# A rotated tile's stack filled by three reads of 32 rows, and the first maxima sent before the last two query tiles

## The reference

```python
q = _apply_rope(q, cos, sin)
k = _apply_rope(k, cos, sin)
k_h = jnp.repeat(k, GROUP_SIZE, axis=1)
v_h = jnp.repeat(v, GROUP_SIZE, axis=1)
scores = jnp.einsum('bhqd,bhkd->bhqk', q, k_h) / math.sqrt(HEAD_DIM)
scores = jnp.where(causal[None, None], jnp.finfo(scores.dtype).min, scores)
attn = jax.nn.softmax(scores, axis=-1)
ctx = jnp.einsum('bhqk,bhkd->bhqd', attn, v_h)
```

## Time and profile before

| | before |
|---|---|
| median of 3 runs | 604.18 us (604.08 to 607.48) |
| the profiled execution | 602.86 us, span 601.1 us |
| mean granted TensorE clock | 0.936 |
| TensorE busy (matmuls) | 475.4 us, 79% |
| VectorE busy | 364.4 us, 61% |
| ScalarE busy | 300.8 us, 50% |
| POOL busy | 280.6 us, 47% |
| DMA moved | 50.83 MB, mean 85 GB/s |

### The profile page before, as it was taken

The page is one execution under the profiler, slowest core; times in us unless marked ns, Lnnn a source line. Parts: engine busy times, 40 slices in busy tenths (PEclk is TensorE's granted clock), DMA queues, the critical chain, the costliest instruction groups (busy, mean ns, idle before and its releaser), DMA issues.

```text
span 601.1 us, 9842 instructions
## 1 busy us (share of the span) xinstructions
PE 475.4 (79%) x3986; PEld 264.5 (44%) x3986; DVE 364.4 (61%) x620; ACT 300.8 (50%) x300; POOL 280.6 (47%) x153
## 2 busy tenths in 40 slices
PE   2678987593069899999995888898889999966777
PEld 2356733241035455555552455454444544435433
DVE  5776366673016676676663566687557676767436
ACT  2644224200057556677664577767762641455433
POOL 4030115332037778988886367666773534220000
PEclk9899989797569899999999899999999999997699
DMA  8623264322210111111114022222229110000015
GB/s 327 226 89 99 73 216 152 121 69 71 80 34 11 37 34 41 37 45 46 45 38 130 12 89 91 89 89 89 78 101 332 53 36 17 1 2 1 19 52 213
DMA packets 20424, 50.83 MB, mean 85 GB/s; under 512 B 4248, under 2 KB 9496, under 8 KB 19096
## 3 DMA queue, kind: packets, MB, share of 16 engines
q1 hardware_dynamic: 19080, 41.69, 20.3%
q10 hardware_dynamic: 1296, 8.45, 4.1%
HBM read 40.57 MB, written 9.44 MB: 83 GB/s over the span
## 4 chain that ended last, share of the span: by engine, by line
PE 40%; DVE 16%; ACT 15%; DMA 13%; issue 12%; POOL 2%; SPq 1%; ACTq 0%; DVEq 0%; POOLq 0%
ACT s1reg L510 8%; PE ps L1263 8%; PE ps L1129 6%; PE ps L1191 4%; PE ps L1210 4%; PE ps L1398 4%; DMA qstack<-mrow 4%; DMA rope_scratch<-s1reg 3%; PE ps L1355 3%; PE ps L1171 3%; DVE stat L706 3%; DVE mt L762 2%; DMA qstack<-rope_scratch 2%; PE ps L1157 2%; DMA s1reg<-in_weights 2%
## 5 line engine op out<-in xcount | busy, mean ns | idle before, releaser
L762 DVE TENSOR_REDUCE mt<-ps 128x1 f32<-128x512 f32 (+3 forms) x176 | 107.2, 637 | 118.7 <-PE ps L1173 118.1
L510 ACT ACTIVATE s1reg<-ps 128x1280 f32<-128x1280 f32 x64 | 78.7, 1229 | 67.5 <-PE ps L1193 66.7
L1129 PE MATMUL ps<-xT,wqx 128*128 128x512 f16 x384 | 98.0, 393 | 7.1 <-DVE s1reg L753 7.1
L1191 PE MATMUL ps<-qstack,kreg 98*128 98x512 f16 (+3 forms) x256 | 59.3, 309 | 54.0 <-DMA qstack<-mrow 28.5
L1263 PE MATMUL ps<-wo_reg,xT 128*128 128x512 f16 x384 | 93.1, 383 | 7.8 <-DVE wqx L790 6.9
L1171 PE MATMUL ps<-kreg,qstack 96*128 96x512 f16 (+3 forms) x256 | 67.2, 309 | 10.3 <-DMA qstack<-rope_scratch 6.5
L1059 POOL TENSOR_TENSOR s1reg<-s1reg 128x1280 f16<-128x1280 f32 x19 | 49.8, 2629 | 33.8 <-ACT s1reg L516 33.8
L1191 PEld LDWEIGHTS ps<-qstack,kreg 98*128 98x128 f16 x256 | 25.5, 100 | 82.0 <-ACT s1reg L510 33.9
L1129 PEld LDWEIGHTS ps<-xT,wqx 128*128 128x128 f16 x384 | 36.2, 101 | 47.1 <-issue 14.0
L1263 PEld LDWEIGHTS ps<-wo_reg,xT 128*128 128x128 f16 x384 | 35.7, 98 | 46.1 <-DVE wqx L790 7.1
L1059 POOL TENSOR_TENSOR wkv<-s1reg,wkv 128x1280 f16<-128x1280 f32 x18 | 46.9, 2615 | 19.3 <-ACT wkv L516 19.3
(11 more groups left out here) (128 smaller groups left out, 939.5 us busy)
## 6 DMA issues: line engine op xcount, KB each, us to landing
s1reg<-in_weights ACTq DMA_DIRECT2D x8, 1024.0 KB, 6.2
s1reg<-in_ctx SPq DMA_DIRECT2D x16, 512.0 KB, 4.7
rope_scratch<-s1reg SPq DMA_DIRECT2D x40, 128.0 KB, 2.5
qstack<-in_x SPq DMA_DIRECT2D x8, 512.0 KB, 5.4
qstack<-rope_scratch SPq DMA_DIRECT2D x16, 256.0 KB
s1reg<-in_x SPq DMA_DIRECT2D x16, 256.0 KB, 3.1
out<-s1reg SPq DMA_DIRECT2D x7, 512.0 KB, 2.7
s1reg<-in_L_ffn_weight SPq DMA_DIRECT2D x5, 512.0 KB, 5.8
```

What stands on the lines that cost most here:

```text
L510: nc.scalar.activation(ebuf[:, j % 2, :], st_ps[:, 0:SCORES], ACT.Exp, scale=EXP_SCALE, bias=P_LOG_SCALE).then_inc(e_done, 1)
L762: nc.vector.reduce_max(mt[:, G % 2, heads[0]:heads[-1] + 1, qt:qt + 1], ps[:, 3 + n % 2, 0:w * len(heads)].rearrange("p (h n) -> p h n", n ...
L1129: last = mm(out_ap, w(ws, k), xT[:, xs, KT * b + k, :], start=(k == 0 and n == 0), stop=(k == KT - 1 and n == 2))
L1191: mm(st_ps[:, SEG[k]:SEG[k] + n], kstack[0:ST_ROWS, one(G), P * k:P * k + P], qstack[0:ST_ROWS, one(slot + j), P * k:T], start=True, stop= ...
```

## The change

A stack is filled by three reads of 32 rows x 4 KB, one for each part, all of the form that so far only the last part had; `from_scratch` takes the list of the halves. The counts on `stack_ready` go from 32 to 48 for a tile. And `maxima(0)` stands ahead of tiles 10 and 11 on SyncE's queue, where it stood between them.

```diff
-            def from_scratch(n, to, slot, pair):
+            def from_scratch(n, to, slot, parts):
                 sp.wait_ge(scr_written[n % 2], 32 * (n // 2 + 1))
                 if n >= 2:
-                    sp.wait_ge(stack_ready[n % 2], 32 * (n // 2))
-                sp.dma_start(to[0:2 * DH, slot:slot + HG, :], pair).then_inc(stack_ready[n % 2], 16)
+                    sp.wait_ge(stack_ready[n % 2], 48 * (n // 2))
+                for part, hl in enumerate(parts):
+                    sp.dma_start(to[DH * part:DH * part + DH, slot:slot + HG, :], scr[n, :, hl, :, :]).then_inc(stack_ready[n % 2], 16)
 
             def k_stack(n):
-                from_scratch(n, kstack, HG * n, scr[n, :, 0:1, :, :].rearrange("r s h t -> s r (h t)").broadcast_to([2, DH, HG * T]))
-                sp.dma_start(kstack[2 * DH:QK_ROWS, HG * n:HG * n + HG, :], scr[n, :, 1, :, :]).then_inc(stack_ready[n % 2], 16)
+                from_scratch(n, kstack, HG * n, (0, 0, 1))
 
             def q_stack(n):
-                slot = (n - 4) % KV * HG
-                from_scratch(n, qstack, slot, scr[n, :, :, :, :].rearrange("r s h t -> s r (h t)"))
-                sp.dma_start(qstack[2 * DH:QK_ROWS, slot:slot + HG, :], scr[n, :, 0, :, :]).then_inc(stack_ready[n % 2], 16)
+                from_scratch(n, qstack, (n - 4) % KV * HG, (0, 1, 0))
...
-            to_scratch(10)
-            q_stack(10)
             maxima(0)
-            to_scratch(11)
-            q_stack(11)
+            for n in range(10, 12):
+                to_scratch(n)
+                q_stack(n)
...
-                    pe.wait_ge(stack_ready[G % 2], 32 * (G // 2 + 3))
+                    pe.wait_ge(stack_ready[G % 2], 48 * (G // 2 + 3))
```

## The result

| | before | changed |
|---|---|---|
| median of the runs | 604.13 us (604.01 to 607.48) | 561.41 us (559.44 to 561.94) |
| the profiled execution | 602.86 us, span 601.1 us | 559.44 us, span 557.6 us |
| mean granted TensorE clock | 0.936 | 0.971 |
| TensorE busy | 475.4 us | 472.1 us |

The ratio, which is estimated from all the runs, is 0.9275 (95% interval 0.9236 to 0.9313), so 43.8 us less, between 41.5 and 46.2; the two medians alone are 42.7 us apart. The forecast was 36.1 us less.

The account below looks back on a forecast made before the run. TensorE was taken to wait on the tiles' transport, paced by 64-row reads on two DMA engines. Gains of 25.3 + 9.3 + 1.0 + 0.5 = 36.1 us off 604.18 gave 568.1 us, range 561 to 580.

Parts of the forecast that it names:

- The two-engine read as the pace of the transport: SyncE's stack transport: the 64-row read runs on two DMA engines, 9.05 us a tile; three reads make it 5 us.
- 25.3 us for the maxima: TensorE's wait for the first row of maxima: goes in full, 25.3 us gained, with a cover of 2.5 us.
- Tile 4, 9.3 us: Rotation and stack waits at tile 4: 3.3 + 6.5 - 0.5 = 9.3 us gained, between 5 and 9.8.
- Clock, 1.0 us: After tile 4's 6.5 us pause: without it TensorE's clock is not lowered, 1.0 us gained, between 0 and 1.9.
- The first group, 0.5 us: First group after the maxima stall: 0.5 us gained of the 1.3 us it takes above a middle group.
- a group longer than 18 us: Sign of being wrong: any group taking over 18 us, where groups of 16.6 us were expected.
- Later groups: Groups after the first: reads are already issued behind the maxima and nobody waits for them, cost 0.
- only the order counts: Rival at the reads: time goes by bytes or rows, however spread; 8.7 us gained, 595 us, chance 0.04.
- slower: Rival at the reads: all three land on the same two engines; 7.8 us lost, 612 us, chance 0.02.
- Little changed: Rival at the reads: their fixed parts add up and spreading saves nothing; 3.6 us lost, 607.8 us, chance 0.01.
- the new wait at the maxima: Rival: maxima behind the reads, or VectorE, hold TensorE; 5 to 15 us given back, 577 to 590, chance 0.08.
- The range: Predicted total time: 561 to 580 us, holding the forecast and the start of the new-wait rival.

Follow-up runs that it names:

- wide 64-row read: Changed kernel with two reads a tile, 64 rows in one read from a scratch layout with outermost dimension 64, and one of 32: 560.08 us, ratio 0.9257.
- order-only run: Kernel before with the first maxima moved ahead of tiles 10 and 11, the 64-row reads kept: 598.67 us, ratio 0.9874.

## Why the prediction was right or wrong

- **The two-engine read as the pace of the transport**: right. Rate, share and collision came out, and the wide 64-row read shows it without the split. The pace fell to 4.4 us a tile, 5 were worked out.
- **25.3 us for the maxima**: right, the whole wait is gone. They left at 127.6 and landed at 130.1, and TensorE asked at 134.1; they were forecast to be ready at 125.8, to land by 130 and to be asked for at 132.5.
- **Tile 4, 9.3 us**: 6.5 measured (113.90 to 107.37). The load landed at 88.7 as forecast (88.4 to 89). TensorE asked for the stack at 104.7 instead of 104.1 and then waited 2.7 us instead of 0.5. The chain of waits of the changed kernel says where these come from:

```profile
94.79 1.17 POOL s1reg L1039
...
95.97 4.05 DMA rope_scratch<-s1reg
...
100.86 6.46 DMA qstack<-rope_scratch
```

The long add cost less against the forecast than it looks: POOL's low half, counted with the 2.74 us of the kernel before, took 1.17 us and ended at 95.95 instead of 95.4. The larger miss is the landing of the reads: beside weight 9's load, issued at 99.84, the last one took 6.46 us, where 3.6 to 4.2 were counted. The reading of the earlier trace rows was off too, though the conclusion stands: both loads were still under way at 91.4 (they landed at 92.66 and 96.39), so the two engines carried their shares then and not the read alone.
- **Clock, 1.0 us**: the stretch from the first scores to group 0 is 2.2 us shorter apart from the stall (28.9 against 26.7). Mis-sized by 1.2, above its upper bound of 1.9; by luck it filled nearly half of tile 4's gap. The 4.6 us behind the first scores, at 0.56 in the earlier trace rows, now run at 1.00 and hold 23 matmuls instead of 13 (window of the changed kernel):

```profile
107.40:112.00 4.60, 4.60 (x23) 2.15 (x24) 3.35 (x3) 1.85 (x2) 3.70 (x2) 1.00 0.38 127
```

- **The first group, 0.5 us**: group 0 takes 18.13 us against 17.85 before, nothing gained; groups 1 and 2 together gave 1.4, which I had not counted. In the second execution of the changed kernel they gave nothing (36.6 us against 36.0), so this is scatter as much as gain. Groups 0 and 1, at 18.13 and 18.18 us, also meet the prediction's sign of being wrong, "a group longer than 18 us"; it was set too near, since group 1 took 18.24 us before the change already.
- **The step that failed**: "Later groups: the reads are issued behind the maxima there already and nobody waits for them. Cost 0." It asked who waits for the reads, and there nobody does. It did not ask what is issued behind them on the same two engines. That is the first residual tile, behind tile 19's stack, and it was worth 7.0 us in group 9 (8.0 in the second execution). With it the sum is 36.1 + 7.0 = 43.1 us against 43.8 measured (41.5 to 46.2). That it closes so well is partly luck: in the first pair of traces tile 4 (2.8 too much), the clock (1.2 too little), the first three groups (0.6 too little) and the stretch behind group 10 (1.4, scatter of the last stage) nearly cancel.
- **The rivals**: "only the order counts" and "slower" fell with the share of 0.79 and 253 GB/s. The order-only run shows what the first would have looked like: 598.7, with the stall mostly there. "Little changed" fell with the 4.4 us a tile, and the new wait at the maxima did not come.
- **The range**: its lower end was made of bounds for terms that I had seen. The missing term was not a bound but a place. It stood in the trace of before: 10.15 us for 256 KB, whose median is 3.1, is the fourth longest of the 1400 pieces in the chain of waits.

## What to carry to other kernels

When one DMA is slow because it runs on few engines, its price is paid by whatever is issued behind it, here on its own queue (maxima, residual) and on another (the weight load). So look up everything that follows each of its instances in the queue, in the whole program and not only where its own consumer waits, and compare every landing time with the median of its kind. Check the outermost dimension on both sides of a DMA: a dimension of 2 there went with two engines here, and a layout that merged it did as much as the split. And when a load becomes faster, look at what its consumer will then run beside.

## What the runs showed of the hardware

- A read of 256 KB whose source has an outermost dimension of 2 holds two engines at 23 to 26.5 GB/s each (share 0.13, 46 to 53 GB/s); the same 256 KB with an outermost dimension of 64 land in 3.5 us.
- 4 KB issued behind such a read on the same queue took 6.90 and 8.09 us to land instead of 1.8; 256 KB of residual 10.15 and 9.64 instead of 3.1; a weight load of 1 MB on ScalarE's queue 10.51 and 11.0 instead of 6.5.
- POOL's add of 128x512 took 3.3 us when it started 0.1 us behind a step of VectorE with two inputs in SBUF, and 1.26 alone; when it started 0.15 to 0.2 us ahead, it took 1.26 and VectorE's step 3.2 to 3.3 instead of 2.29. I had counted with 1.26 and with no such meeting.
- Three reads of 128 KB issued 0.2 us behind a weight load of 1 MB took up to 6.46 us to land, and at most 2.7 where the load was issued behind them.
